# Decoder layer on one core: attention scores from fp16 high and low parts of the transposed queries and keys

## The reference

```python
q = (x @ w_q.T); k = (x @ w_k.T); v = (x @ w_v.T)          # per head, 64 wide
q, k = rope(q), rope(k)
scores = einsum('bhqd,bhkd->bhqk', q, k)                   # the product that is changed
attn = softmax(where(causal, scores, -1e9) / sqrt(64))
x = layernorm(x + (attn @ v) @ w_out.T)
x = layernorm(x + conv(x, ctx))
x = layernorm(x + ffn(x))
```

## Time and profile before

| | |
|---|---|
| median of three runs | 1454.53 us (1453.53 to 1455.14) |
| profiled execution | 1454.28 us, of which the span of the instructions is 1452.4 us |
| busy share of the span | PE 95%, PEld 48%, DVE 73%, ACT 42%, POOL 16% |
| granted TensorE clock, mean | 0.984 of 2.4 GHz |

### The profile page before, as it was taken

The page is one execution under the profiler, slowest core; times in us unless marked ns, Lnnn a source line. Parts: engine busy times, 40 slices in busy tenths (PEclk is TensorE's granted clock), DMA queues, the critical chain, the costliest instruction groups (busy, mean ns, idle before and its releaser), DMA issues.

```text
span 1452.4 us, 23295 instructions
## 1 busy us (share of the span) xinstructions
PE 1378.8 (95%) x7576; PEld 693.7 (48%) x7576; DVE 1065.1 (73%) x1847; ACT 613.0 (42%) x1203; POOL 232.6 (16%) x270
## 2 busy tenths in 40 slices
PE   6787999999999999999999979999999999999996
PEld 2343555555545545555555544444444444444443
DVE  2896554565477778677778767888888888888884
ACT  4765554654455454446545443222223222222221
POOL 0112122122213222221312211000000000000000
PEclk9898999999999999999999999999999999999999
DMA  9503534454444534444453574222222222222200
GB/s 364 217 2 116 197 138 164 148 173 143 140 149 140 173 126 152 157 125 153 157 178 105 150 234 127 73 75 84 73 72 72 72 72 72 72 72 72 72 20 24
DMA packets 63572, 178.92 MB, mean 123 GB/s; under 512 B 15361, under 2 KB 26673, under 8 KB 63537
## 3 DMA queue, kind: packets, MB, share of 16 engines
q1 hardware_dynamic: 63536, 178.48, 37.8%
HBM read 153.02 MB, written 25.43 MB: 123 GB/s over the span
## 4 chain that ended last, share of the span: by engine, by line
issue 43%; PE 38%; DVE 7%; POOL 4%; DMA 3%; ACT 3%; SPq 1%; POOLq 0%; ACTq 0%; DVEq 0%
PE ps L493 31%; PE ps L484 3%; DMA ctx<-ctx 2%; PE ps L585 2%; PE ps L567 2%; DVE weights L1054 1%; POOL q L1383 1%; ACT tern L858 1%; PE ps L542 1%; POOL simw L1431 1%; POOL k L1361 1%; POOL rstd L1378 1%; DVE weights L1053 1%; ACT prob L778 1%; DMA tern<-conv_w 0%
## 5 line engine op out<-in xcount | busy, mean ns | idle before, releaser
L493 PE MATMUL ps<-weights,xT 128*128 128x512 f16 x2160 | 484.7, 382 | 0.0
L493 PEld LDWEIGHTS ps<-weights,xT 128*128 128x128 f16 x2160 | 209.7, 98 | 242.4 <-issue 10.0
L654 PE MATMUL ps<-weights 128*128 128x512 fp8e4 (+1 forms) x1536 | 300.0, 357 | 0.0
L654 PEld LDWEIGHTS ps<-weights 128*128 128x128 bf16 x1536 | 146.9, 98 | 154.8
L493 PE MATMUL ps<-weights 128*128 128x512 f16 x768 | 170.4, 382 | 6.6 <-ACT v L716 6.2
L878 ACT ACTIVATE weights<-ps,xscale 128x512 f32<-128x512 f32 x96 | 61.7, 643 | 251.6 <-PE ps L654 251.6
L682 PE MATMUL ps<-weights 128*128 128x512 fp8e4 x704 | 157.2, 380 | 0.0
L778 ACT ACTIVATE prob<-prob,negmax,undo 128x128 f32<-128x128 f32 x256 | 122.7, 483 | 14.5 <-DVE negmax L1090 14.5
L493 PEld LDWEIGHTS ps<-weights 128*128 128x128 f16 x768 | 75.4, 98 | 98.5 <-ACT v L716 6.7
L682 PEld LDWEIGHTS ps<-weights 128*128 128x128 bf16 x704 | 67.7, 98 | 75.9 <-issue 0.2
L1378 POOL TENSOR_TENSOR rstd<-rstd,expo 128x1 f32<-128x1 f32 x32 | 17.3, 541 | 532.8 <-DVE rstd L983 532.8
(11 more groups left out here) (151 smaller groups left out, 1797.7 us busy)
## 6 DMA issues: line engine op xcount, KB each, us to landing
wch<-w_ffn SPq DMA_DIRECT2D x96, 688.0 KB, 4.3
wch<-sim_scratch SPq DMA_DIRECT2D x96, 128.0 KB
ternary_scratch<-tern SPq DMA_DIRECT2D x48, 172.0 KB, 1.9
ctx<-ctx SPq DMA_DIRECT2D x16, 512.0 KB
wo_raw<-x_scratch SPq DMA_DIRECT2D x16, 512.0 KB, 3.3
out<-k SPq DMA_DIRECT2D x16, 512.0 KB, 2.7
x_in<-xT_in SPq DMA_DIRECT2D x15, 512.0 KB, 6.8
weights<-x SPq DMA_DIRECT2D x15, 512.0 KB, 10.6
```

The lines of the kernel that those rows point to most:

```text
L493: ins = nc.tensor.matmul(ps[:, bank], partsT[:, a, t], weights[:, t, w, half * HALF:(half + 1) * HALF], start=(t == 0 and a + w == 0), sto ...
L654: ins = nc.tensor.matmul(ps[:, 2 * w + a, 0:n], xqT[:, t], w8m[:, t, at:at + n], start=(t == 0), stop=(t == KT - 1))
```

## The change

`qkT` becomes fp16 with one more index: high (0) and low (1) part. ScalarE's copy (`high_bank`, in place of `copy_bank`) writes the high part as fp16 and sets `qkT_high`. VectorE (`qkT_low`) then subtracts the high part from the same PSUM bank, writes the low part and sets `tr_free`. `scores(u)` makes three fp16 products (high by high, high by low, low by high) where one fp32 product stood, 24 instructions in a step. `qkT_low(0)` stands at the start of VectorE's turn, ahead of rope(b+1, 0), and `qkT_low(1)` right behind mask_max(0); in turn 15 ahead of residual(0, 0) and between mask_max(0) and scale_x(1).

```diff
-        qkT = sb("qkT", [P, 2, 4, P], F32)
+        qkT = sb("qkT", [P, 2, 2, 4, P], F16)
...
+        qkT_high = sem("qkT_high")
...
                     for t in range(4):
-                        for r in range(2):
-                            ins = nc.tensor.matmul(ps[:, SC + r, t * P:(t + 1) * P], qkT[64 * r:64 * r + 64, 0, t],
-                                                   qkT[64 * r:64 * r + 64, 1, t], start=True, stop=True)
+                        for a, w in ((0, 0), (0, 1), (1, 0)):
+                            for r in range(2):
+                                rows = slice(64 * r, 64 * r + 64)
+                                ins = nc.tensor.matmul(ps[:, SC + r, t * P:(t + 1) * P], qkT[rows, a, 0, t],
+                                                       qkT[rows, w, 1, t], start=(a + w == 0), stop=(a == 1))
                     ins.then_inc(scores_full, 1)
...
+                def high_bank(w, u):
+
+                    act.wait_ge(tr_full[w], tr_pair(b, u) + 1)
+                    nc.scalar.copy(qkT[:, 0, w], ps[:, TR + w].rearrange("p (t n) -> p t n", t=4)).then_inc(qkT_high, 1)
...
                 for w in range(2):
-                    copy_bank(w, tr_pair(b, 0), qkT[:, w])
+                    high_bank(w, 0)
                 square_wo(0, 2)
                 act.wait_ge(scores_full, b * 2 + 1)
                 for w in range(2):
-                    copy_bank(w, tr_pair(b, 1), qkT[:, w])
+                    high_bank(w, 1)
...
+                def qkT_low(u):
+
+                    for w in range(2):
+                        dve.wait_ge(qkT_high, b * 4 + (2 * u + w + 1))
+                        nc.vector.tensor_tensor(qkT[:, 1, w], ps[:, TR + w].rearrange("p (t n) -> p t n", t=4), qkT[:, 0, w],
+                                                ALU.subtract).then_inc(tr_free[w], 1)
+
...
                 def turn_last():
+                    qkT_low(0)
                     residual(0, 0)
                     norm_sums(x2n)
                     mask_max(0)
+                    qkT_low(1)
                     scale_x(1)
...
+                qkT_low(0)
                 rope(b + 1, 0)
                 mask_max(0)
+                qkT_low(1)
```

## The result

The changed kernel takes 1458.79 us (median of seven runs, 1455.84 to 1460.72) against 1454.77 us for the kernel before, run beside it: a ratio of 1.0026 [1.0016, 1.0037], so 4.0 us slower. The profiled execution took 1459.43 us, 5.15 more than the one before.

A forecast was written before the change was run, and what follows sets the result against it. The prediction took the context load's chain to pv(0) to bound most loop turns, and VectorE's work turns 0 and 15. Sum: 1454.28 - 1.4 + 2.6 + 1.2 + 1.7 = 1458.4 us, range 1455.0 to 1464.0.

The forecast's parts named there:

- The products overlap: Scores steps: fp16 products on the two row groups run side by side, 0.84 us a step, a gain of 0.25.
- The first rival: Scores steps: the fp16 pairs don't overlap, each step is 0.35 us longer, total 1465.7 us; chance 0.14.
- The context chain sets pv(0) in the loop: Loop turns: norm, store, loads, ctx_square, sign_chunk and copies set pv(0), without scores; gain 0 in turns 7 to 12.
- The second rival: Turns 1 to 14: TensorE's time counts and the low parts hide, 8.0 us gained, total 1446.3 us; chance 0.07.
- The cap of 0.4 us at prob_T(0): Loop turns: prob_T(0) needs normalise(0), so at most 0.4 of the 0.50 us of two steps is left there.
- The loop's sum: Turns 1 to 14: gains of 1.1 us in turns 1 to 5 and 13 and 0.3 in turn 6, -1.4 us.
- the margin: Turns 1 to 5 and 13: how far TensorE comes last at pv(0) behind ScalarE's copies, 1.1 us in all.
- The low parts hide in turns 1 to 14: VectorE's low parts fit into its waits there and cost nothing; scores(0) has 0.9 us to spare.
- Turn 0: Nothing hides the two low parts of 1.2 us each on VectorE there: +2.6 us, bounds 2.4 and 3.0.
- The rival in which turn 0 gives back its shift: Turn 0's waits at its end absorb the 2.6 us shift, total 1455.8 us, no change; chance 0.12.
- Turn 15: qkT_low(1) delays normalise(0) and so prob_T(0), +1.2 us; a slower clock behind the longer idle adds 1.7.
- a fall of the clock: Turn 15: TensorE's idle grows from 2.18 to some 3.3 us, its clock falls behind it, +1.7 us, bounds 0 and 1.7.

The follow-up runs named there:

- e3: Changed kernel with one score product in place of three in all turns, low parts still written: 1457.73 us.
- e5: Kernel before, with the context load issued earlier, between the two weight chunks: 1449.31 us.
- e6: Changed kernel with the context load issued earlier, between the two weight chunks: 1449.70 us.
- e4: Changed kernel with fp32 scores and the old copy in turns 0 and 15: 1453.75 us.
- e7: Changed kernel with normalise(0) ahead of scale_x(1) in turn 15: 1458.71 us.
- e8: Changed kernel with qkT_low(0) of turn 0 ahead of four of the six last value weight splits: 1457.62 us.
- e10: Changed kernel with fp32 scores and the old copy in turn 15 alone: 1456.40 us.
- e11: Changed kernel with fp32 scores and the old copy in turn 0 alone: 1455.34 us.
- e2: Changed kernel without low parts in turns 1 to 14, scores there three products of the high parts: 1458.30 us.
- e1: Changed kernel without low parts in turns 0 and 15, scores there three products of the high parts: 1453.22 us.
- e9: Changed kernel with fp32 scores in turns 0 and 15 and the context load ahead of the second weight chunk: 1444.75 us.
- e12: As e9, with scale_x(1) of turn 15 behind normalise(0) besides: 1443.43 us.

## Why the prediction was right

Forecast 1458.4 us with the sign slower; measured 1458.79. Step by step:

**The products overlap.** 0.84 us a step was forecast, 0.78 measured. The first rival (no overlap, 1465.7) falls: 24 instructions in 0.78 us are 0.033 each. The Trainium skill, "TensorE: Matmul & The Clock Gate", Part 1, has about 62 ns for each where the sequencer's firmware decodes them; the trace disagrees with that as a rule for this kernel, with these 0.033 us.

**The context chain sets pv(0) in the loop.** Right, and shown: e3 takes off TensorE's work and pv(0) stays, e5 takes off the load and pv(0) comes earlier. The second rival (TensorE's time counts, 1446.3) holds only in the loop and only once the load is moved, as in e6. The cap of 0.4 us at prob_T(0) by normalise(0) is seen as the idle of 0.17 there, in e3 as 1.07; and 0.40 a turn is what e6 gains over e5.

**The loop's sum.** Forecast -1.4 us, in the trace -0.16 for turns 1 to 13 and -0.69 for turn 14, which I had put at 0 with a bound of 0.4. In turn 14 the bound failed: over all traces it takes 38.4 us in the mean with fp16 scores (twelve traces, 37.63 to 39.07) and 39.0 with fp32 (before 39.14, e5 38.84), so about all that two steps save (2 x 0.31) comes through there. Turns 1 to 6 gave -1.6, near the forecast, and turns 7 to 13 gave +1.4 where I had 0. I don't take that for an effect of the change: e4, e7, e8, e10 and e11 have the same loop, and their turns 1 to 13 take 650.9, 652.5, 654.7, 651.7 and 654.1 us. With the 654.1 of the kernel after that is 653.0 in the mean, 1.3 below the one trace of the kernel before.

The landing of the context load sets these turns, and it varies: in turn 8 ctx_square starts 13.58 us after the end of the norm before, in the kernel after 13.01 (from 501.29 to 514.30). Taken from the length of the turn (end of norm to end of norm) this leaves the same remainder in both kernels (us; "ctx_square" is its start, counted from the end of the norm before):

| turn | ctx_square before | turn before | remainder | ctx_square after | turn after | remainder |
|---|---|---|---|---|---|---|
| 8 | 13.58 | 50.49 | 36.91 | 13.01 | 49.92 | 36.91 |
| 10 | 13.22 | 50.13 | 36.91 | 13.89 | 50.80 | 36.91 |
| 12 | 13.13 | 50.04 | 36.91 | 13.83 | 50.73 | 36.90 |

It is 36.90 or 36.91 in turns 7 to 12 of the kernel before and in turns 7 to 13 of the kernel after: each 0.1 us of a later landing is 0.1 us of turn, and the scores are not in it. In other traces single turns take up to 0.8 us more than that (e3, turn 8: 37.73): there one VectorE instruction ahead of the norm, the scaling of x, takes 2.44 us in place of 1.28. In turns 1 to 5 the kernel before takes 49.67 or 49.68 us whatever the landing, so TensorE, which comes last at pv(0) there, sets them; in the kernel after the landing sets these too (remainder 36.51 or 36.52), which is why they gain only the margin. What moves the landing wasn't tried.

```profile
514.30 1.16 ACT L801 ACTIVATE sq<-ctx 128x1152 f32<-128x1152 f32 x1 [3.79 <-DMA ctx<-ctx]
```

(Timeline of ScalarE, turn 8, kernel after.)

**The low parts hide in turns 1 to 14.** Right (e2). scores(0) has 1.02 us to spare, 0.9 was forecast.

**Turn 0.** Forecast +2.6, +2.43 in the trace; but VectorE's part of the turn began 0.35 us earlier in the kernel after (84.69 against 85.04), so it lost 2.78 from there, within the bounds of 2.4 and 3.0. The other traces agree: from VectorE's first split of the value weights (73.12 before, 72.77 after) to the end of the norm, the seven with low parts in turn 0 take 76.79 to 78.54 us, 77.44 in the mean, the seven without 74.11 to 75.69, 74.65 in the mean: 2.8 us. The wait for the first low part and the half clock behind it (0.50 in 82.3 to 88.9) came as described, and the rope covered them but for 0.34 us at mask_max(0), inside the bound of 0.6 (timeline of VectorE, kernel after):

```profile
87.58 0.69 DVE L1100 TENSOR_TENSOR prob<-ps,maskb 128x512 f32<-128x512 f32 x1 [0.34 <-PE ps L570]
```

The rival in which turn 0 gives back its shift falls by e11: without the low parts of that turn 3.5 us are gone by the medians.

**Turn 15.** Forecast 1.2 for the low part and 1.7 for a fall of the clock; +3.38 in the trace. From the convolution to prob_T(0) 17.41 us pass, 16.30 before: 1.11 for the low part. From prob_T(0) to the end of the projection 7.96 (860.66 + 6.93 - 859.63) and 6.26 before: 1.70 for the clock. Behind prob_T(1) another 0.57, which I had left out: the clock fell there in the kernel before too, but one step later (its pv(1), not its prob_T(1), took 1.97 or 1.98). So in this pair of traces both terms came out at their forecast sizes.

The cause that I gave for the fall is not shown, though, and the 1.7 us are not what it costs on average. I put it down to the idle growing from 2.18 to 3.3 us. Of the seven traces with a low part in turn 15 six show the fall at prob_T(0) or right behind it, and e7 shows one at prob_T(1); but of the seven without it (before, e1, e4, e5, e9, e10, e12) four show it as well: e1 after an idle of 2.80 us, and e4, e5 and e10 after the 2.17 or 2.18 us behind which the clock held in the kernel before and in e9. Each time the two steps take 7.7 to 8.0 us in place of 6.3. By the idle ahead of prob_T(0): after 3.22 to 3.66 us all six fell, after 2.17 to 2.80 four of six, after 1.24 and 1.40 (e7, e12) neither. So the longer idle may make the fall likelier. It does not decide it: in turn 0 the clock fell in the kernel before after an idle of 3.34 us and held in e5 after 3.33 (projection 5.34 us). And the trace that I compared with was one of the two at 2.2 us in which the clock held. The Trainium skill says on "TensorE: Matmul & The Clock Gate", Part 1, that the hardware's look at TensorE's activity runs freely and doesn't start anew with a kernel, and that the point at which the clock rises therefore differs from run to run. Three falls in five traces at an unchanged idle would agree with the same for falls; no run here shows the reason.

The mis-sized term is thus the fall of the clock, which the forecast put at its full price against a trace without one. From the start of scores(0) of turn 15 to the first product of phase 2, the six traces with the low part and the order of the change take 38.84 to 39.75 us (mean 39.3, the kernel after 39.70); the six without it in that order take 36.32 to 38.72 (mean 37.6, the kernel before 36.32, the shortest). That is 1.7 us in the mean where I had 1.2 + 1.7 = 2.9, and of the 1.7 VectorE's work is 1.1, so that some 0.6 is left for the clock. e10's gain (2.4 by the medians, 0.9 by the ratios) fits it.

**The total** was nearer than its terms, and in part that is luck: in the two profiles the ends cost 5.8 us where I had 5.5 and the loop gave 0.85 where I had 1.4; over the traces turn 15 costs 1.2 us less than I had and turn 14 gives 0.6 that I had not. The medians are 4.0 us apart, and the interval of the ratio reaches from 2.3 to 5.4.

## What to carry to other kernels

Before work is moved from the busiest engine to another, look for the step at which that engine waits in each stage, and for what ends the wait: here a load issued late in the DMA queue's order took most of the gain in turns 1 to 13, and moving it by one place made the same change worth 0.40 us a turn there. To see whether a wait that varies sets a stage, take the end of the wait from the stage's length, turn by turn: here the remainder was the same to 0.01 us in every one of these turns, in both kernels. A cost that hides in the steady state still shows in the first and the last turn, where other work fills the helping engine; the old form can stay there. Here three fp16 products paid against one in fp32 only in the turns where the engine that makes the parts had time to spare. And where the clock falls in some executions and not in others, one trace is no base for a forecast: several are needed.

## What the runs showed of the hardware

Three fp16 products of 64 rows by 128 columns on two row groups take less time together (0.78 us a step) than one in fp32 (1.09), each with its own weight load. The subtraction that makes the low part from PSUM costs VectorE 0.683 us for 128x512, as the line's group of the kernel after shows (count, busy us, mean ns, idle before):

```profile
L1091 DVE TENSOR_TENSOR qkT<-ps,qkT 128x512 f16<-128x512 f32 x64 | 41.0, 683 | 0.0
```

So 41.0 us of VectorE buy 32 x 0.31 = 10 us of TensorE's steps (its busy time fell by 7). And TensorE's clock fell to its 1.2 GHz level after idles of about 2.2 us in some executions (e4, e5, e10) and not in others (before, e9) with the same instructions in that turn.
